# Writing out the loop over three Fourier layers, on every engine, in a Trainium2 kernel

## What is computed

```python
h = layer_norm(x @ fc0_w + fc0_b, ln0_g, ln0_b)
for i in range(4):
    x1 = spectral_conv(h, w1[i], w2[i])          # rfft2, mix 2 x 12 x 12 modes over channels, irfft2
    x2 = einsum('bchw,oc->bohw', h, conv_w[i]) + conv_b[i]
    h = layer_norm(x1 + x2, ln_g[i], ln_b[i])
    if i < 3: h = gelu(h)
h = gelu(h @ fc1_w + fc1_b); h = gelu(h @ fc2_w + fc2_b); h = h @ fc3_w + fc3_b
```

## Time and profile before

| what | value |
|---|---|
| median of 3 runs | 4682.74 us (4681.69 to 4684.64) |
| the profiled execution | 4677.02 us, of which the span is 4675.2 us |
| granted TensorE clock, mean | 0.935 |
| PE, PEld, DVE, ACT, POOL busy | 83%, 64%, 50%, 45%, 17% |
| span from 400.29 to 3641.19 us | four groups; the loop over l takes some 510 us in each |
| span from 3862.4 us on | the four blocks after the tokenizer |

### The profile page before, as it was taken

How to read it: one execution, slowest core, us unless ns; L and a number is a source line. 1 busy time by engine, 2 the same in 40 slices (tenths; PEclk the granted TensorE clock), 3 DMA queues, 4 the chain that set the end, 5 groups by cost and what they waited for, 6 DMA issues and landing times. The chain is left out here.

```text
span 4675.2 us, 102193 instructions
## 1 busy us (share of the span) xinstructions
PE 3900.5 (83%) x39344; PEld 2983.1 (64%) x39344; DVE 2320.5 (50%) x5028; ACT 2091.3 (45%) x3178; POOL 809.9 (17%) x540
## 2 busy tenths in 40 slices
PE   0089999998899999979999999799999995686168
PEld 0058888852788888337888873478888724572056
DVE  6564454532545445234544551354454503968756
ACT  1154454456545444664544547554454481230012
POOL 0031131220213112111311320122122300001020
PEclk9989999999999999989999999899999997688679
DMA  8501111110022020100211201021120001000000
GB/s 203 179 25 63 43 62 63 42 55 4 22 75 70 22 83 22 56 3 22 83 63 39 66 22 56 3 75 30 64 82 22 22 2 32 1 1 0 0 1 10
DMA packets 168551, 208.67 MB, mean 45 GB/s; under 512 B 156386, under 2 KB 158663, under 8 KB 159858
## 3 DMA queue, kind: packets, MB, share of 16 engines
q1 hardware_dynamic: 166370, 178.13, 13.3%
q10 hardware_dynamic: 1680, 23.60, 2.0%
HBM read 142.57 MB, written 59.12 MB: 43 GB/s over the span
## 5 line engine op out<-in xcount | busy, mean ns | idle before, releaser
L767 POOL TENSOR_TENSOR rstd<-var,mhalf 128x16 f32<-128x16 f32 x240 | 698.9, 2912 | 38.9 <-POOL var L764 17.6
L744 ACT ACTIVATE h<-tp,gb 128x512 f32<-128x512 f32 x640 | 554.1, 869 | 277.2 <-PE tp L465 275.4
L708 DVE TENSOR_REDUCE ssum<-sq 128x16 f32<-128x512 f32 x640 | 432.2, 682 | 300.7 <-ACT sq L732 298.0
L764 POOL TENSOR_TENSOR var<-ssum,eps 128x16 f32<-128x16 f32 x240 | 52.4, 218 | 2942.2 <-DVE ssum L708 2942.2
L465 PE MATMUL tp<-ident,xn 128*128 128x128 f32 x2560 | 418.2, 289 | 104.2 <-DVE xn L699 86.2
L457 PEld LDWEIGHTS main<-convw,h 128*128 128x128 f32 x3072 | 378.5, 196 | 150.4 <-issue 150.4
L506 PE MATMUL main<-fwd_w,pix 128*128 128x96 f32 x4096 | 464.8, 276 | 7.0 <-ACT pix L598 7.0
L506 PEld LDWEIGHTS main<-fwd_w,pix 128*128 128x128 f32 x4096 | 459.8, 192 | 10.3 <-DVE pix L598 8.6
L732 ACT ACTIVATE sq<-main 128x512 f32<-128x512 f32 x480 | 287.5, 602 | 346.2 <-PE main L457 238.4
L465 PEld LDWEIGHTS tp<-ident,xn 128*128 128x128 f32 x2560 | 304.0, 147 | 198.3 <-DVE xn L699 170.9
L424 PE MATMUL aux<-inv_r,yd 96*48 96x64 f32 x8192 | 421.1, 257 | 6.9 <-DVE zq L598 3.3
(11 more groups left out here) (240 smaller groups left out, 5944.6 us busy)
## 6 DMA issues: line engine op xcount, KB each, us to landing
mixw<-mix_scratch SPq DMA_DIRECT2D x15, 4608.0 KB, 14.8
y_scratch<-t_w SPq DMA_DIRECT2D x256, 144.0 KB
yd<-y_scratch SPq DMA_DIRECT2D x32, 1152.0 KB, 7.1
mix_scratch<-mixw SPq DMA_DIRECT2D x64, 288.0 KB, 4.7
mixw<-mix_scratch ACTq DMA_DIRECT2D x1, 4608.0 KB, 13.7
h<-in_L_tok_w1r ACTq DMA_DIRECT2D x6, 576.0 KB, 9.7
h<-in_L_tok_w1i ACTq DMA_DIRECT2D x6, 576.0 KB, 10.1
h<-in_L_tok_w2r ACTq DMA_DIRECT2D x6, 576.0 KB, 18.4
```

The lines of the kernel that those rows point to most:

```text
L708: dve.tensor_reduce(ssum[:, c % 4, :], sq[:, c % 2, :].rearrange("p (n c) -> p n c", c=CH), AX.X, ALU.add).then_inc(red_done, 1)
L744: act.activation(out, in_, fn, bias=gb[:, 1, stage:stage + 1] if l is None else gb[:, 1, bass.ds(stage, 1)], scale=gb[:, 0, stage:stage + ...
L767: pool.tensor_tensor(rstd[:, c % 4, :], var[:, c % 4, :], mhalf[:, :], ALU.pow).then_inc(rstd_done, 2)
```

## The change

The loop over l becomes three copies of its body on PE, DVE, ACT, POOL and SP. In each copy l is a number, so that addresses and counts that had a register for l have a constant for it; those with g keep their register. The loop over the groups stays, with its branch at the end of `mlp`. The instructions that compute or move data, and their order, stay the same.

```diff
@@ -828,7 +828,7 @@
         def program(eng, embed, layer, last, mlp):
             with eng.Fori(0, GROUPS) as g:
                 embed(g)
-                with eng.Fori(0, LAYERS - 1) as l:
+                for l in range(LAYERS - 1):
                     layer(g, l)
                 last(g)
                 mlp(g)
@@ -916,7 +916,7 @@
                 def layers(g):
                     for u in range(UNITS):
                         sp_spectrum(sp, g, 0, u, None)
-                    with sp.Fori(0, LAYERS - 1) as l:
+                    for l in range(LAYERS - 1):
                         for u in range(UNITS):
                             if u == 0:
                                 sp.wait_ge(main_full, base_of(g, 1, 0, l)[0] + NCH // 2)
```

## The result

| what | before | changed |
|---|---|---|
| median | 4682.22 us (4679.83 to 4684.64, 4 runs) | 4619.76 us (4617.84 to 4626.73, 4 runs) |
| ratio to before, 95% interval | | 0.987 [0.9855, 0.9886] |
| profiled execution: time, span | 4677.02, 4675.2 | 4617.89, 4616.1 |
| the loop over l, four groups | 2042.60 | 1982.06 |
| table loads at L732, L744 | 12, 12 | 0, 4 |

The changed kernel is faster by 62.5 us in the medians, and by 59.1 in the profiled executions, where 57 was forecast; in the loop over l it is 60.5. The median forecast was 4626, with 4616 to 4645 as its range.

What follows compares the result with a forecast made beforehand. PE was taken to bound the loop. A body of 55.9 us, plus 1.6 for untaken branches, less 0.8 for the kept table load, gave 56.7, say 57, and a median of 4626 us, range 4616 to 4645.

Steps and rivals of the forecast that it cites:

- The body of the sum: Loop over l: its measured 2042.60 us less 24 clean unit periods of 82.78 us, a gain of 55.9 us.
- The clean period: Loop over l: a unit period without stall, slow clock or table loads, taken as 82.78 us.
- Stalls: Start of l = 1 and 2: PE idle at its taken branch, some 35 us in the four groups.
- Slow clock and tables: Unit 0 periods: half clock after the stall plus ACT's table loads, some 21 us in the four groups.
- The kept load of L744: ACT at l = 0: the table load that remains takes 0.8 us off the gain, bounds 0 and 2.5.
- the share of the second load: ACT's load at L744: about 0.15 to 0.2 us of a period's 0.63, the first load taking 0.48.
- The untaken branch: PE in each of 24 periods: 83 ns removed, 2.0 us in all, of which 1.6 was taken; bounds 0 and 2.0.
- What is late next: Start of l = 1 and 2: spectrum and mix weights stay covered with PE some 4.3 us sooner, costing nothing.
- Unit 0 that stays long (2): Unit 0 periods: stalls go but the periods stay long, only some 35 us gained, median 4647; chance 9%.
- Straight code that starves an engine (3): Loop periods: late code stalls about 4.2 us; once in each period gives 4727; chance 2%.
- Tables in full (4): Loop over l: 20 table loads wholly on PE's path, 25.7 us, gain about 78, median 4605; chance 3%.
- The 4594: Whole time if 20 removed loads, at the page's price on PE's path, were worth 53 us beside the stalls.

Runs made afterwards that it cites:

- The mirror: Against the changed kernel, ACT, DVE, POOL and SP keep the loop over l and PE alone runs the three copies: 4629.68 us.
- the memsets that moved it: Against the changed kernel, 15 or 74 one-element memsets put ahead of DVE's program, so its code stands later: 4628.62 us with 15, 4629.04 with 74.

## Why the prediction was right

**The body of the sum.** 2042.60 - 24 x 82.78 gave 55.9; the loop gave 60.5. The method held. The clean period was taken too long: 82.34, not 82.78. Of the 0.44 us, 0.36 is one long step of DVE at L668 in every period of unit 1 of the kernel before, which I didn't see. The other 0.08 is what the correction had in it, a branch that isn't taken, or the 0.07 us by which L454 and L539 overlap where nothing stands between them. The mirror has the long step and no branch on PE, and its unit 1 takes 82.70. The long step would have been worth 24 x 0.36 = 8.6 us, and the changed kernel gives 1982.06 - 24 x 82.34 = 5.9 us back in long steps of its own. 55.9 + 2.0 + 8.6 - 5.9 = 60.6. Neither the 8.6 nor the 5.9 was in my sum, and that they cancel to 2.7 us is luck.

**Stalls**, some 35 us: right, and PE's alone. **Slow clock and tables**, some 21 us: too small. The twelve periods of unit 0 lie 25.8 us over 82.34. I gave the tables 0.63 us in a period. They cost 1.04: the 82.78 of unit 1 that I took off held the 0.36 of a long step, and unit 0 has none. **The kept load of L744**, 0.8 us: it costs nothing; the mis-sized term is the share of the second load, all of the cost is the first's. **The untaken branch**, 1.6 us of 2.0: nearly all of it. (2, 1) takes 82.78 us before and 82.70 in the mirror, where PE alone has lost the branch. The bounds of 0 and 2.0 held.

**Costs don't add.** Against the changed kernel, PE alone in the loop costs 57.0 us of loop time, ACT alone 12.7, DVE alone 2.8: 72.5. All together, as before, cost 60.5. Behind the stall PE runs at half clock, and the loads hide there: (1, 0) is 85.27 with tables and 85.00 without. DVE's branch, 4.4 us alone, stands behind the same stall.

**What is late next**: nothing, as said. Spectrum and weights stayed covered; at 4.3 us sooner no wait appeared ahead of L424 or L539 in the loop.

**The rivals.** Unit 0 that stays long (2) fell by the windows. Straight code that starves an engine (3) fell as a stall of 4 us, but the long steps of DVE show that something of the kind exists at a tenth of the size. Tables in full (4) fell: 12.7 us and not 25.7. In the Trainium skill, ScalarE: Activation LUTs, "What ACT_TABLE_LOAD costs", the load's 1,283 ns agree with every row; its drain of 1,380 ns is in none, and the first square follows 1.30 us after the load's start. The 4594 that I worked out from the page's price leaves out the 17 us of slow clock that the fourth rival's own sum has.

**Against the whole time**: 60.5 us in the loop became 59.1 in the span. PE's branches at the groups' ends got longer, two of three by over 1 us (up to 5.0 us against at most 3.9), but that isn't the cause: the wait for ACT's copy covers them, and from the last L592 to L447 are 11.6 to 11.7 us in both kernels. The 1.4 us are the sum of shifts of up to 2 us each way in `last`, `mlp`, `embed` and what stands before and behind the groups. In the medians the gain is 62.5, above the 52 to 60 that I gave the gain itself. As what stands outside the loop differs by up to 21 us among the kernels above, a whole time within 7 us of the forecast is luck in part; the loop's 60.5 for 57 is what the method can claim.

## What to carry to other kernels

Look for matmul engines that stand still with "issue" as the releaser at the same place in each iteration: a loop whose body is long costs its far branch and the slow clock after it, here 4.4 + 2.5 us a time, while a near branch costs 0.3. When parts of a kernel repeat exactly, take the shortest clean repetition for the unit price, and look at why the others are longer before you multiply; a repetition with nothing late in it need not be a floor. An activation table load was free ahead of a wait for data and cost 1.04 us behind it. With the first iteration written out, the loop that was left loaded no table at all.

## What was not expected of the hardware

- DVE has a step that starts 0.16 to 0.36 us late at fixed places of its program. In the kernel with all groups written out they are at records 576, 832, 960, 1216 and 1600: 256, 128, 256 and 384 apart, multiples of 128. PE feels one only where it falls in the serial chain, and not every one there. That it is a seam of fetched code is argued from the spacing, from the memsets that moved it, and from the instruction packets: in the kernel before, a q14 packet of 8 KB starts 0.59 to 0.69 us behind 23 of the 24 long steps in DVE's chains, and 0.95 behind the other. Which of the two waits for what no row shows.
- POOL's branch back was near 0.25 us while its body was short; with the longer body of the changed kernel the next instruction comes 2.5 us later. It had over 100 us of slack. The length decides. Counted in the trace's records from the target to the branch, the next instruction comes after 0.16 us over 72 (POOL) and 0.24 to 0.28 us over 217 (POOL) and 305 (ACT), but after 2.4 to 2.7 us over 354 (POOL) and 926 (ACT), and 2.8 to 3.1 over 487 (DVE).
- The table load of 1.28 us cost PE 1.04 us behind a wait for data, nothing ahead of it, and nothing at L744, in the same kernel body.
